# Decoder layer on one core: out_proj and w_o as three products of rounded halves, buffers shared or used in place, and new call lists

## The reference, cut to what matters

```python
# per sequence; x: (256, 256), ctx: (120, 256)
x = layernorm(x + mamba(x))
x = layernorm(x + cross_attention(ctx, x))
x = layernorm(x + coupling_ffn(x))

# mamba: z, xBC, dt from x @ W_in.T; causal conv of 4 taps and silu on xBC; state space sum over tokens
y = ssd(x * dt, A * dt, B, C) + x * D           # 8 heads of 64
y = y * silu(z)
y = y * rsqrt(mean(y * y) + 1e-5) * norm_w
return y @ W_out.T                              # 512 -> 256: out_proj

# cross attention: keys and values from [norm(ctx); norm(x)] (376 rows), 8 heads of 64
out = softmax(q @ k.T) @ v
return out @ Wout                               # 512 -> 256: w_o

# ffn: three cycles of a small gelu network (tf), one global gate (gf)
out = out + coupling(gf, tf) * twist(out)
```

## Time and profile before

| what | us |
|---|---|
| median of three runs | 3997.05 |
| lowest and highest | 3990.07, 4003.43 |
| the profiled execution's own time | 3990.73 |
| its span, first to last instruction | 3988.9 |

### The profile page before, as it was taken

How to read it: one execution, slowest core, us unless ns; L and a number is a source line. 1 busy time by engine, 2 the same in 40 slices (tenths; PEclk the granted TensorE clock), 3 DMA queues, 4 the chain that set the end, 5 groups by cost and what they waited for, 6 DMA issues and landing times.

```text
span 3988.9 us, 77174 instructions
## 1 busy us (share of the span) xinstructions
PE 3836.7 (96%) x25984; PEld 3029.0 (76%) x25984; DVE 3195.2 (80%) x7215; ACT 3184.6 (80%) x7739; POOL 1742.9 (44%) x2824
## 2 busy tenths in 40 slices
PE   4999999999999999999999999999999999999996
PEld 3777777777777777777777777777777777777774
DVE  6688888888888888888888888888888888888863
ACT  3788888888888888888888888888888888888873
POOL 2344444444444444444444444444444444444431
PEclk7999999999999999999999999999999999999997
DMA  2121121121121121121121111111111111111110
GB/s 92 33 62 53 41 62 53 41 62 53 41 62 51 42 62 50 44 60 51 45 58 52 46 55 55 46 53 57 46 53 57 46 53 57 46 53 57 46 31 14
DMA packets 311801, 203.13 MB, mean 51 GB/s; under 512 B 54768, under 2 KB 310640, under 8 KB 311408
## 3 DMA queue, kind: packets, MB, share of 16 engines
q1 hardware_dynamic: 311408, 198.20, 17.1%
...
## 4 chain that ended last, share of the span: by engine, by line
PE 77%; SPq 6%; DMA 5%; DVE 5%; ACT 4%; issue 3%; POOL 0%; DVEq 0%; ACTq 0%; POOLq 0%
PE psum L247 26%; PE psum L428 9%; PE psum L438 8%; PE psum L452 7%; PE psum L463 6%; PE psum L338 6%; DMA invT<-inv_row 5%; PE psum L325 5%; PE psum L497 3%; SPq L1649 3%; PE psum L503 2%; ACT L780 2%; SPq L1666 2%; DVE oT L1217 1%; ACT prob L780 1%
## 5 line engine op out<-in xcount | busy, mean ns | idle before, releaser
L780 ACT ACTIVATE prob<-psum,nmax 128x376 f32<-128x376 f32 x1024 | 585.7, 573 | 134.6 <-DVE nmax L1189 114.4
L1189 DVE TENSOR_REDUCE nmax<-psum 128x1 f32<-128x376 f32 x1024 | 533.8, 537 | 121.0 <-PE psum L428 121.0
L1476 POOL TENSOR_TENSOR Lm<-Lm,G 128x768 f32<-128x768 f32 x256 | 490.3, 1915 | 255.0 <-ACT Lm L717 255.0
L438 PE MATMUL psum<-ident,prob 128*128 128x128 f32 (+1 forms) x3072 | 496.6, 277 | 2.0 <-ACT probT L790 1.3
L1013 DVE SCALAR_TENSOR_TENSOR u<-psum,par,u 128x255 f32<-128x255 f32 (+5 forms) x960 | 449.3, 479 | 29.5 <-ACT u L658 3.3
L428 PE MATMUL psum<-kT,q_sb 64*128 64x376 f32 x2048 | 466.2, 528 | 2.1 <-ACT q_sb L753 1.4
L438 PEld LDWEIGHTS psum<-ident,prob 128*128 128x128 f32 (+1 forms) x3072 | 364.5, 143 | 126.3 <-issue 94.2
L452 PE MATMUL psum<-probT,V 128*64 128x256 f32 (+1 forms) x3072 | 388.5, 387 | 1.3 <-ACT probT L790 1.0
L1530 POOL TENSOR_TENSOR h_a<-h_a,cpl 128x512 f32<-128x512 f32 x64 | 89.0, 1390 | 679.5 <-DVE h_pre L1275 679.5
L247 PE MATMUL psum<-x_hi,w_in_hi 128*128 128x256 f32 (+1 forms) x1152 | 349.7, 304 | 22.3 <-DVE x_lo L1009 19.6
L1208 DVE COPY probT<-psum 128x384 f32<-128x384 f32 x512 | 280.7, 548 | 68.1 <-PE psum L438 66.1
...
## 6 DMA issues: line engine op xcount, KB each, us to landing
...
invT<-inv_row SPq DMA_DIRECT2D x256, 128.0 KB, 3.0
xT_sb<-in_xT SPq DMA_DIRECT2D x64, 256.0 KB, 3.1
x_sb<-in_x SPq DMA_DIRECT2D x64, 256.0 KB, 3.4
result<-out_sb SPq DMA_DIRECT2D x64, 256.0 KB, 2.2
inv_row<-inv_t SPq DMA_DIRECT2D x512, 1.0 KB
...
```

The source lines that it names most:

```text
L438: t = tr(banks[b][0:m, j * P:(j + 1) * P], prob[:, r, j0:j0 + m], ident[:, :])
L780: act(prob[:, r, :], b[:, 0:NK], ACT.Exp, bias=nmax[:, n:n + 1], accum_out=psum_row[:, n:n + 1]).then_inc(a_exp, 1)
L1189: e.tensor_reduce(nmax[:, n:n + 1], banks[bank_of["sc", s, n]][:, 0:NK], AX.X, ALU.max, negate=True).then_inc(d_max, 1)
L1476: tt(pair, pair, G[:, :].unsqueeze(1).broadcast_to([P, 2, TRI]), ALU.mult).then_inc(l_Lm, 1)
```

## The change

- **out_proj and w_o.** Both become product3 with the activation as the stationary side. out_proj is 24 matmuls where the trace showed 16, w_o 12 where it showed 8. g and oT are rounded into one shared pair r_hi, r_lo: g_high and o_high (DVE, a copy of 128x512, two calls each) and g_low and o_low (POOL, a subtraction of 128x512, two calls each) are new. W_out and W_o are split at the start on DVE, four pairs of copy and subtraction of 128x256 each.
- **Space.** The rings of prob and probT go from 7 to 6 and 6 to 5 places; x_sb has one place; g is xc, ctx_n is ctx_sb, x1_n is x1_pre, dt_a is Bz, dt_e is th. x1_keep now comes before x1_norm, and x1T waits for both. xT and x have semaphores of their own; load_ctx waits for ctxT, load_x for x1_raw of the sequence before.
- **Lists.** All five lists have a new order.

Its core:

```diff
-    NP, HP = 7, 6
+    NP, HP = 6, 5
-        w_out_sb, wo_sb = sb("w_out_sb", [P, CT, D]), sb("wo_sb", [P, CT, D])
+        w_out_hi, w_out_lo = sb("w_out_hi", [P, CT, D], F32R), sb("w_out_lo", [P, CT, D], F32R)
+        wo_hi, wo_lo = sb("wo_hi", [P, CT, D], F32R), sb("wo_lo", [P, CT, D], F32R)
...
-        g = sb("g", [P, CT, L])
-        yD, sq = xc, gate
+        yD, g, sq = xc, xc, gate
+        r_hi, r_lo = sb("r_hi", [P, CT, L], F32R), sb("r_lo", [P, CT, L], F32R)
+        x1_n, ctx_n = x1_pre, ctx_sb
...
             def out_proj(s):
-                pe.wait_ge(l_g, 4 * s + 4)
+                pe.wait_ge(d_ghi, 2 * s + 2)
+                pe.wait_ge(l_glo, 2 * s + 2)
                 for i in range(TT):
-                    for c in range(CT):
-                        t = mm(banks[b][:, i * D:(i + 1) * D], g[:, c, i * P:(i + 1) * P], w_out_sb[:, c, :],
-                               start=c == 0, stop=c == CT - 1)
+                    ti = slice(i * P, (i + 1) * P)
+                    t = product3(banks[b][:, i * D:(i + 1) * D], [w_out_hi[:, c, :] for c in range(CT)],
+                                 [w_out_lo[:, c, :] for c in range(CT)], [r_hi[:, c, ti] for c in range(CT)],
+                                 [r_lo[:, c, ti] for c in range(CT)], x_is_rhs=False)
...
             def w_o(s, i):
-                pe.wait_ge(d_o, 2 * s + 2)
+                pe.wait_ge(d_ohi, 2 * s + 2)
+                pe.wait_ge(l_olo, 2 * s + 2)
...
             def x1_keep(s):
+                ve.wait_ge(l_mix, 3 * s + 3)
...
+            def g_high(s, d):
+                ve.wait_ge(l_g, 4 * s + 2 * d + 2)
+                ve.wait_ge(p_wo, 2 * (s - 1))
+                cp(r_hi[:, 2 * d:2 * d + 2, :], g[:, 2 * d:2 * d + 2, :]).then_inc(d_ghi, 1)
+            def o_high(s, d):
+                ve.wait_ge(d_o, 2 * s + d + 1)
+                ve.wait_ge(p_out, min(s + 2, NSEQ))
+                cp(r_hi[:, 2 * d:2 * d + 2, :], oT[:, 2 * d:2 * d + 2, :]).then_inc(d_ohi, 1)
...
+            def g_low(s, d):
+                po.wait_ge(d_ghi, 2 * s + d + 1)
+                tt(r_lo[:, dd, :], g[:, dd, :], r_hi[:, dd, :].bitcast(F32), ALU.subtract).then_inc(l_glo, 1)
+            def o_low(s, d):
+                po.wait_ge(d_ohi, 2 * s + d + 1)
+                tt(r_lo[:, dd, :], oT[:, dd, :], r_hi[:, dd, :].bitcast(F32), ALU.subtract).then_inc(l_olo, 1)
...
             def load_xT(s):
+                sp.wait_ge(d_xlo, s)
+                e.dma_start(xT_sb[:, :, :], xT[s].rearrange("(k p) t -> p k t", p=P)).then_inc(xT_in[s % 2], 16)
```

More of the change, by code:

```diff
@@ L1387, in _ @@
                 top(a, 12)
-                top(a, 13)
+                g_high(m, 0)
                 bcdt(m + 1)
-                turn_out(a, 6)
-                top(a, 14)
-                softplus(m + 1)
+                x2_split(f)
+                g_high(m, 1)
                 conv(m + 1, 0)
                 conv(m + 1, 1)
-                x2_split(f)
-                mean_square(m)
-                top(a, 15)
-                x1_raw(m)
-                turn_out(a, 8)
-                kv_split(m, 0)
@@ L1401, in _ @@
-                turn_out(a, 10)
-                x1_norm(m)
-                conv(m + 1, 2)
-                conv(m + 1, 3)
-                cum(m + 1)
-                bc(m + 1)
+                turn_out(a, 8)
+                softplus(m + 1)
+                context(m + 1)
+                top(a, 13)
+                turn_out(a, 10)
+                kv_split(m, 0)
+                mean_square(m)
+                top(a, 14)
+                x1_raw(m)
+                cum(m + 1)
+                conv(m + 1, 2)
@@ L1442, in _ @@
-                top(m, 7)
+                x2_raw(a, 0)
+                turn_out(m, 2)
+                y_out(m + 1, 0)
+                gate_silu(m + 1, 1)
+                top(m, 4)
+                top(m, 5)
+                out_sum(f, 1)
+                out_sum(f, 0)
+                top(m, 6)
+                out_stats(f, 0)
+                x2_raw(a, 1)
+                out_stats(f, 1)
+                x2_stats(a, 1)
+                top(m, 7)
+                out_norm(f, 0)
+                top(m, 8)
@@ L1445, in _ @@
+                out_norm(f, 1)
+                x2_stats(a, 0)
+                top(m, 9)
+                y_out(m + 1, 1)
+                turn_out(m, 4)
+                inverse(m, 0)
+                top(m, 10)
+                top(m, 11)
+                y_out(m + 1, 2)
+                x2_norm(a, 1)
         @block.gpsimd
```

410 lines of the change are left out of this document (210 added, 200 removed).

## The result

The changed kernel takes 4091.47 us (median; 4086.72 to 4092.68) against 3997.09 us of the kernel before on the same chip: ratio 1.0234, 95% interval [1.0215, 1.0253]. Forecast were 3964 us, with 3900 to 4040 as the range: wrong in sign, and outside the range.

What follows compares the result with a forecast made beforehand. PE's own list plus one gap was taken as the bound. On the profiled execution 3990.7 - 80 + 62 x (1.1 + 0.35 - 0.8) + 6 = 3957; with 6.3 for the median, 3964 us, range 3900 to 4040.

Steps and rivals of the forecast that it cites:

- PE's own list: PE's matmuls in out_proj and w_o: shorter by 1.25 us a pass, 80 us in all.
- The rival that the products don't run at in_z's pace: out_proj and w_o on PE: new products slower than in_z's matmuls of the same shape and type; chance 0.01.
- the wait at w_o goes: PE ahead of w_o: its 0.8 us wait a pass disappears, with 0.4 us or more to spare.
- nine table loads a pass: ACT: nine function-table loads a pass instead of six, 3.9 us more work a pass.
- The shorter rings, the single x_sb and the buffers used in place: Buffer space: costs nothing; if the cover were gone, each such wait would be one turn, 0.33 us.
- one g_high more (0.43): DVE between w_o and the next x2_split: one added cast of 0.43 us, within 19.6 us busy.
- rival 4: DVE becomes the bound between w_o and x2_split: two more writes held by POOL, 0.7 each; 4051 us; chance 0.14.
- The wait at bcdt behind x_low: PE at bcdt or layer(f,0,0), waiting for DVE: 1.1 us a pass, between 0 and 2.9.
- ACT and x1T: ACT from glob 1 to layer(f,0,1), with the x1 chain: 0.35 us a pass, between 0 and 1.3.
- rival 5: ACT at layer(f,0,1) or layer(f,1,0): one added table load uncovered, 1.3 us a pass; 4045 us; chance 0.09.
- Rival 2: All covered: DVE keeps up, PE's waits at or below 0.5; about 3903, up to 3935 us; chance 0.22.
- Rival 3: The gains cancel: PE's waits are 1.9 to 2.2 us a pass; 3985 to 4009 us; chance 0.12.

Runs made afterwards that it cites:

- the bank: Changed kernel with glob(f, 1) and mean_square written into glob(f, 0)'s psum bank instead of the next in the ring: 4054.2 us.
- the cast: Changed kernel with DVE's g_high(m, 1) moved from ahead of conv(m + 1, 0) to between conv(m + 1, 0) and conv(m + 1, 1): 4036.8 us.
- the subtractions, or o_high and o_low, are reduced: Two runs of the changed kernel writing 2 of 256 columns after the first sequence: g_low and o_low, 4035.4 us; o_high and o_low, 4036.3 us.
- the halves reduced, the bank reused and the loads away: Changed kernel, four helpers on 2 of 256 columns, glob(f, 1) and mean_square in glob(f, 0)'s bank, softplus's Exp and Ln as Squares: 3975.5 us.
- moving the taps: DVE's conv(m + 1, 2) put behind x1_keep and x1_norm: 4027.0 us with plain products, 4099.6 us in the changed kernel with glob(f, 0)'s bank reused.

## Why the prediction was wrong

**Right: PE's own list.** out_proj runs from 2043.87 to 2046.78, 2.91 us, and each w_o takes 1.50 (2016.75 to 2018.25). Together, from start to start, 5.91 against 7.12 a pass (3.56, 1.83 and 1.73 before, read the same way): 1.21 saved where 1.25 was forecast. The rival that the products don't run at in_z's pace is out.

**Right: the wait at w_o goes; nine table loads a pass.** No wait at w_o is left in a full pass. The loads are 565 in all, 9 a pass, 1283 ns each.

**Failed: no term for the psum banks.** "The shorter rings, the single x_sb and the buffers used in place I cost at nothing": I checked the rings of prob and probT and the buffers of x, and not the ring of two psum banks that in_x, glob and mean_square share, whose order the new list changes. There the new order hands glob(f, 1) the bank of in_x(m + 1, 0), which DVE's taps free. This wait alone is 0.95 us a pass, and taking it away gave 37 us (the bank), or taking away three quarters of it 55 us (the cast).

**Failed: "one g_high more (0.43)".** The stretch of DVE was summed with free durations. The cast that counts is held up to 1.52 us by POOL's squares, and it stands directly ahead of the taps: 1.1 us at the one place where DVE has no slack. The same holds for Cz (+0.97 a pass), divide (+0.71) and x2_norm (+0.53), where the xcT wait comes from: it is gone where the subtractions, or o_high and o_low, are reduced, with Cz back at 429 ns in the first of these. I had named the mechanism in rival 4 and its stretch, but priced it by a mean over rows, 0.7 an instruction, and never asked which DVE instruction stands beside which of POOL's and what is queued behind it.

**Half right: bcdt and ACT.** The wait at bcdt behind x_low came, 0.55 instead of 1.1. ACT and x1T were put at 0.35 and are 0.60 + 0.27. The stretch that I had compared was the right one: ACT from glob 1 to the end of layer(f, 0, 1) at 6.8 "at most", PE at 6.4. ACT takes 7.25 from glob(f, 1)'s start. So rival 5's mechanism, a load that isn't covered, came at layer(f, 0, 2), and it takes back what the shorter out_proj saves in this stretch, 0.65 of the 1.21. Rivals 4 and 5 were priced as alternatives. They came together, behind a third link, the bank, that I had not seen.

**The sum by what was measured.** Forecast was a pass of 59.36 (59.96 - 1.25 + 1.1 + 0.35 - 0.8). By the waits it is 59.96 - 1.21 - 0.8 + 2.8 = 60.75; 61.65 was measured. Most of the 0.9 between is the view itself: a wait counts from the modelled end of the matmul ahead, which lies about 0.15 behind the point at which the next one starts when it is free to (2047.64 beside 2046.78 + 1.02). There are five more waits a pass than before, so 0.75. That part is an estimate, and the last 0.15 isn't located.

**Slips in the forecast's own sums.** The sum gives 3963, not 3964. Rival 2's 3903 is its price with the full 0.5 of waits; with none it would be 3873, below the range. Rival 3's 1.9 would be 3992, its 3985 belongs to 1.8. None of these changes the outcome.

**What stays open.** With the halves reduced, the bank reused and the loads away, PE still waits 1.3 us a pass, 0.65 of it at x1T. That it comes from conv 2's taps and x1_keep ahead of x1_norm is likely, as moving the taps removed it, but no run removed it without a new wait. Nor was the cast moved off squares together with ACT's loads taken away, which would say whether these two are all that glob(f, 1) and layer(f, 0, 2) lose. g_high behind POOL's squares, the bank reused and w_o plain, all three together, weren't tried; whether such a version beats plain products isn't known. Of what was run with nothing left out, plain products under the new lists are the fastest, 3983.6 us, 0.36% below the kernel before. Their pass is no shorter (3903.7 - 181.3 over 62 is 60.04, against 59.96); by their first load the start is 8 us shorter.
